# A four-layer graph network on one core: units of two slots of seven destination tiles in place of groups of four slots of one tile

## What is computed

```
layer 0: two graph attentions (4 heads, self loops added):
    e = leaky_relu(alpha_s[src] + alpha_d[dst]); softmax of e over the edges of each dst
    out[dst] = sum of alpha * h[src] + bias          (elu between the two)
layer 1: relu(x W_self + b) and relu((sum of weight * x[src] by dst) W_neigh + b), normalized, added
layer 2: attention with q, k, v (8 heads) over the same edges and loops, batch norms, feed-forward
layer 3: e = (h[dst] - h[src]) theta + h[src] phi; relu(bn(e)); e fc1; relu(bn(e)); mean over the edges of dst; relu(x + h)
```

## Time and profile before

| what | us |
| --- | --- |
| median of three runs (lowest, highest) | 13634.71 (13632.43, 13640.51) |
| profiled execution, its span | 15925.7 |
| order_nodes, build_slots (0 to 1190) | 696 and 494 |
| first gather pass, layer 0 (1369 to 4600) | 3231 |
| second gather pass, layer 0 (4725 to 7944) | 3219 |
| layer 1 and the setup of layer 2 (7944 to 9142) | 1198 |
| third gather pass, layer 2 (9142 to 11728) | 2586 |
| fourth gather pass, edge_stats (12207 to 14745) | 2538 |
| edge_spread (14745 to 15197) | 452 |
| edge_mean (15197 to the end) | 729 |

### The profile page before, as it was taken

One profiled execution on the slowest core, in us unless ns is written; L12 is line 12 of the kernel. 1 busy time (PEld: TensorE's weight loads), 2 busy tenths in 40 slices (PEclk: granted clock), 3 DMA queues, 4 the chain that ended last, 5 costly groups with the idle time before them and its releaser, 6 DMA issues. The chain is left out here.

```text
span 15925.7 us, 135557 instructions
## 1 busy us (share of the span) xinstructions
PE 3804.3 (24%) x15373; PEld 2322.4 (15%) x15374; DVE 8054.8 (51%) x18639; ACT 2750.8 (17%) x7793; POOL 7318.6 (46%) x7722
## 2 busy tenths in 40 slices
PE   2011112122221112222268200000032111111876
PEld 1001111111221111111234100000011111111321
DVE  8663555555644555555620466666653333333754
ACT  0410222222321222222300000000000000000754
POOL 0105554555545555555400266666623666666024
PEclk9996555555555555555689555555565555555999
DMA  0002222223322222223345133333311332333754
GB/s 2 14 23 48 65 65 69 71 69 76 76 64 63 63 71 64 69 75 76 79 178 219 37 93 93 93 93 95 96 37 52 91 90 89 92 89 89 245 183 147
DMA packets 977545, 1355.17 MB, mean 85 GB/s; under 512 B 223796, under 2 KB 654618, under 8 KB 964536
## 3 DMA queue, kind: packets, MB, share of 16 engines
q0 software_dynamic: 262304, 622.51, 15.4%
q1 hardware_dynamic: 226200, 403.02, 7.7%
q10 hardware_dynamic: 488960, 328.91, 7.1%
HBM read 1006.43 MB, written 347.39 MB: 85 GB/s over the span
## 5 line engine op out<-in xcount | busy, mean ns | idle before, releaser
L819 POOL DMA_INDIRECT ring<-gat_table,index x3424 | 3332.4, 973 | 2981.8 <-POOLq L102 1999.4
L819 POOL DMA_INDIRECT ring<-kv_table,index x1712 | 1693.3, 989 | 868.9 <-issue 431.8
L819 POOL DMA_INDIRECT ring<-b_table,index x1712 | 1629.3, 952 | 956.4 <-issue 522.3
L1045 DVE TENSOR_REDUCE acc<-prod 128x132 f32<-128x660 f32 (+1 forms) x1284 | 1708.0, 1330 | 5.0
L949 PE MATMUL pairs<-hot_lo,hot_hi 128*128 128x128 f32 x6272 | 961.8, 327 | 2317.5 <-ACT hot_lo L976 2070.7
L1033 DVE TENSOR_TENSOR prod<-ring,p 128x528 f32<-128x528 f32 (+1 forms) x1284 | 916.5, 714 | 963.7 <-issue 711.0
L976 ACT ACTIVATE hot_lo<-hot_lo,wt 128x128 f32<-128x128 f32 x3136 | 951.2, 392 | 2021.9 <-DVE hot_lo L929 1699.4
L949 PEld LDWEIGHTS pairs<-hot_lo,hot_hi 128*128 128x128 f32 x6272 | 931.7, 240 | 2375.5 <-issue 2373.5
L1105 ACT ACTIVATE p<-x 128x20 f32<-128x20 f32 (+1 forms) x1284 | 290.7, 226 | 5217.6 <-DVE x L1051 4105.7
L943 PE MATMUL pairs<-nil 128*128 128x512 bf16 x784 | 390.3, 598 | 2790.8 <-issue 1763.5
L1637 PE MATMUL bt<-ident,ring 128*128 128x128 f32 x1712 | 464.9, 427 | 2060.9 <-PEq L102 738.3
(11 more groups left out here) (358 smaller groups left out, 8692.7 us busy)
## 6 DMA issues: line engine op xcount, KB each, us to landing
dense_weights<-dstage ACTq DMA_DIRECT2D x196, 1024.0 KB
mat<-dense_weights SPq DMA_DIRECT2D x98, 1568.0 KB
kept<-tb ACTq DMA_DIRECT2D x432, 256.0 KB
layer_out<-kept SPq DMA_DIRECT2D x428, 256.0 KB
at<-kept SPq DMA_DIRECT2D x428, 256.0 KB
ring<-gat_table,index POOLq DMA_INDIRECT x3424
ring<-kv_table,index POOLq DMA_INDIRECT x1712
ring<-b_table,index POOLq DMA_INDIRECT x1712
```

The costliest lines, as they stand in the source:

```text
L819: pool.indirect_dma_start(self.ring[:, r * J + j, :], None, self.table, bass.IndirectOffsetOnAxis(self.index[:, half, at:at + 1], 0)).then ...
L1045: return dve.tensor_reduce(acc[:, :], prod[:, :, :].rearrange("p s c -> p c s"), AX.X, ALU.add)
```

## The change

Seven tiles form a **band** (NB = 7 bands). A **unit** is S = 2 slots of all seven tiles: UG = 14 gathers, slot by slot. A band has as many units as its highest degree needs, at least seven; the total is rounded up to 4n + 2. The ring holds RU = 4 units (56 gathers). Indices are loaded two units at a time, in three parts of the partitions. `attention_pass` treats a unit in one go: the loop that had the scores of one group beside the products of the one before is replaced by a straight order, and the sum of five by three additions and products over 924 columns (952 in layer 2, where the product with the query is written over the keys in the ring). The dense chunks of layer 0 stand inside the band: each tile's chunk comes ahead of that tile's share of the units (`beside`), its nine waits are two, and the drain behind it is gone. ACT takes a tile's chunk, the exponents of its units, and then its store.

In layer 3 a unit of 917,504 bytes is turned, kept and loaded again, with two buffers (`KeptUnits`) in place of eight; its statistics go over four quarters of 448 columns, and `edge_mean` sums straight into a band's `acc`, so that fold and transpose come once a band. `build_slots` runs over bands and writes `slot_src` in three parts and `turned` in two ("kept edge rows" for up to 160 units; `Regathered` stays for more).

```
-J = 4
-R = 4
-RING = 2 * R
+S = 2
+UG = S * B7
+RU = 4
...
-GMAX = E // J + 4 * T + T * GC + 2 * GC
-CAP = 512
+UMAX = E // S + 256
+CAP = 160
...
 class Gather:
...
+        self.ring = s.sb("ring", [P, RU * UG, width])
...
+            claim(pool, self.i_sem[half], 16 * len(SPARTS))
+            for r in range(half * 2, half * 2 + 2):
+                claim(pool, self.used)
+                for i in range(UG):
+                    at = (r % 2) * UG + i
+                    pool.indirect_dma_start(self.ring[:, r * UG + i, :], None, self.table,
...
 class DenseRows:
...
-        with dve.Fori(c0, c0 + n):
-            take(dve, self.col_in, 16)
-            for b in range(QUADS):
-                take(dve, self.used[b])
+        with dve.Fori(0, n):
+            claim(dve, self.col_in, 32)
+            claim(dve, self.used, QUADS)
...
-            c(dve.drain())
-            c.reset()
...
 def attention_pass
...
+            def unit(u):
+                claim(dve, ga.landed)
+                got = ga.unit(u)
+                for f in scores(dve, got, e[:, 0:S, :], work):
+                    c(f())
+                c(dve.tensor_reduce(newmax[:, :], e[:, :, :].rearrange("p s h -> p h s"), AX.X, ALU.max))
...
                 claim(dve, p_ready)
...
-                dve.tensor_tensor(by_head(prod[:, 0:J, :]), by_head(ga.group(g)[:, :, 0:VB]),
-                                  p5[:, 0:J, :].unsqueeze(3).broadcast_to([P, J, heads, dim + 1]),
+                dve.tensor_tensor(by_head(prod[:, :, :]), by_head(got[:, :, 0:VB]),
+                                  weight[:, 0:UG, :].unsqueeze(3).broadcast_to([P, UG, heads, dim + 1]),
                                   ALU.mult).then_inc(ga.used, 1)
...
+                c(dve.tensor_tensor(by_head(acc[:, :, :]), by_head(acc[:, :, :]),
+                                    weight[:, UG:UG + B7, :].unsqueeze(3).broadcast_to([P, B7, heads, dim + 1]),
+                                    ALU.mult))
+                c(dve.tensor_tensor(prod[:, 0:B7, :], prod[:, 0:B7, :], prod[:, B7:UG, :], ALU.add))
+                dve.tensor_tensor(acc[:, :, :], acc[:, :, :], prod[:, 0:B7, :], ALU.add)
...
-            def add_up():
-                return dve.tensor_reduce(acc[:, :], prod[:, :, :].rearrange("p s c -> p c s"), AX.X, ALU.add)
...
+                    with dve.Fori(b * B7, b * B7 + B7) as t:
+                        rows_of.dve_tile(dve, parts.value())
...
+                        with dve.Fori(u, u + many) as v:
+                            unit(v)
...
-                if rows_of is not None:
-                    rows_of.dve_tile(dve, t)
...
 def edge_stats
...
-        tb = s.sb("tb", [P, R, J * P])
...
+        tb = s.sb("tb", [P, 2, S, W7])
...
-        kept = dram("kept", (CAP + R, P, J * P))
+        kept = dram("kept", (CAP + 2, P, S * W7))
```

More of the change, by code:

```diff
@@ L212, in order_nodes @@
         ti = s.sb("ti", [P, T], I32)
+        band, cnt, run = (s.sb(n, [P, NB]) for n in ("band", "cnt", "run"))
+        bi = s.sb("bi", [P, NB], I32)
+        share, edge = s.sb("share", [P, NB, B7]), s.sb("edge", [P, NB, B7 + 1], I32)
         hist, pre, tots = s.ps("hist", [P, T]), s.ps("pre", [P, T]), s.ps("tots", [P, T])
@@ L337, in _ @@
             dve.wait_ge(md_ready, 1)
[L339 to L368, removed]
@@ new lines, in _ @@
+            c(dve.tensor_tensor(cnt[:, NB - 1:NB], rank[:, 0:1], run[:, NB - 1:NB], ALU.subtract))
+            c(dve.tensor_copy(k.units[:, :], cnt[:, :]))
+            each = cnt[:, :].unsqueeze(2).broadcast_to([P, NB, B7])
+            c(dve.tensor_scalar(k.empty[:, :].rearrange("p (b w) -> p b w", w=B7), each, float(S), None, ALU.mult))
+            c(dve.tensor_tensor(k.empty[:, :], k.empty[:, :], k.deg[:, :], ALU.subtract))
+            c(dve.tensor_tensor(share[:, :, 0:B7], each, k.ramp[:, 0:B7].unsqueeze(1).broadcast_to([P, NB, B7]),
+                                ALU.mult))
@@ L939, in pe @@
         with pe.Fori(0, T) as t:
[L940 removed]
+            n = self.chunks(pe, t)
             for b in range(QUADS):
@@ L1925, in act, with pe_own, pe_unit @@
-    def act(self, act):
-        n = act.value_load(self.k.total[0:1, 0:1], min_val=1, max_val=GMAX)
+    def pe_own(self, pe):
+        take(pe, self.r_ready)
+        for h in range(2):
+            mm = pe.matmul(self.e1[:, h, 0:QW], self.fc[:, :], self.r[:, h * QW:(h + 1) * QW], start=True, stop=True)
+        mm.then_inc(self.e1_ready, 1)
+    def pe_unit(self, pe):
+        for j in range(S):
+            take(pe, self.staged)
+            for w in range(B7):
+                mm = pe.transpose(self.bt[:, w * P:(w + 1) * P], self.stage[:, w, :], self.k.ident[:, :])
+            mm.then_inc(self.turned, 1)
+            self.pe_own(pe)
@@ new lines, in pe_turn, with dve_rows @@
+            def pe_turn(self, pe, a):
+                claim(pe, self.band_done)
+                claim(pe, self.o_free)
+                for w in range(B7):
+                    mm = pe.transpose(o[:, w, :], acc[:, a, w * P:(w + 1) * P], k.ident[:, :])
+                mm.then_inc(self.turned, 1)
+            def dve_rows(self, dve, c, b):
+                rows7, own = y[:, ds(b * B7, B7), :], x[:, ds(b * B7, B7), :]
+                share = rcnt[:, ds(b * B7, B7)].unsqueeze(2).broadcast_to([P, B7, D])
@@ L2147, in _, with unit @@
                 c = Chain(dve, ch)
-                def groups(first, last, q):
-                    with dve.Fori(first, last) as g:
+                def unit(a):
+                    for q in range(2 * S):
                         claim(dve, product)
-                        dve.sem_inc(source.tb_free, 1)
+                        if q == 2 * S - 1:
+                            dve.sem_inc(source.tb_free, 1)
                         dve.sem_inc(source.r4_free, 1)
```

1055 lines of the change are left out of this document (525 added, 530 removed).

## The result

The changed kernel takes 14,930.9 us (median of 4 runs, 14,914.2 to 14,957.5) against 13,637.6 before: a ratio of 1.095, 95% interval 1.0935 to 1.0966. The forecast was slower, 14,287 us, with a range to 14,850; the time lies 81 us above the range. Its profiled execution has a span of 14,912.4 us, within 0.2% of the runs: the 2,291 us by which the profile of before exceeds its runs have no counterpart here.

A forecast was written before the change was run, and what follows sets the result against it. POOL's gathers were taken to bound the four passes, with stalls only about 574 us in a run. Added gathers +540, stalls -434, lock +596 and other stages -50 made +652 on 13,635: 14,287 us, range 13,500 to 14,850.

The forecast's parts named there:

- the lock: Gather passes: a gather starting while VectorE runs a product with two SBUF operands waits for that product's end; new loss 780 us.
- the second loss: First two passes: behind `prod`, a gather start may meet the third 1.12 us product, costing 0 or 0.93, weighed a quarter.
- the work and load of a buffer: edge_spread and edge_mean: load 3.0 to 4.5 us, work some 3.8 us, taken as 4.2 us a unit.
- The frame: Four gather passes: the profile's extra 2,291 us is stalls; runs take 9,283 us there, with only 574 us stalled.
- Rival A: Gather passes: the profile's extra time lies in the 0.30 us gaps, so the kernel gets faster, some 12,100 us; chance 14%.
- +540 for added gathers: Four gather passes: 1,820 gathers a pass against 1,712, at 1.25 us each, if POOL is the bound: +540 us.
- -434 for stalls: Gather passes: 574 us of stalls removed, 140 us added for first and last units of the passes: -434 us.
- +596 for the lock: First three passes: longer two-operand products delay gathers by 780 us, the old 184 gone: +596, bounds +200 and +1,220.
- The row product: First two passes: `prod` of 2.08 us delays the gather it catches by 0.71 to 1.96 us, 1.33 in the middle.
- -50 for the other stages: Outside the passes: build_slots -50, edge_spread +123 to 575 us, edge_mean -127 to 602: -50, bounds -250 and +200.
- Rival C: Gather passes: every unit meets the third product and all gathers under a dense chunk, +1,220, giving 14,911 us; chance 12%.
- Rival B: Gather passes: long gathers belong to two very long products alone; no change, 13,691 or 13,507 us; chance 8%.

The follow-up runs named there:

- e3: Changed kernel with edge_spread and edge_mean loading kept units in halves through five buffers instead of whole units through two: 14,369.1 us, 562 less.

## Why the prediction was wrong

The direction was right, and so was the mechanism of the largest loss, the lock; the size was not: +652 us forecast, +1,296 measured. Two terms were mis-sized: the second loss in a unit of the first two passes, and the work and load of a buffer in the edge stages. By its steps:

- **The frame.** That the profile's 2,291 us extra stand on the stalls at the tiles' ends, and that the runs have only some 574 us of them, fits: POOL no longer stops, and by this sum the runs gained little by it. The stages that the change left alone are as long in both profiles (layer 1 and the setup of layer 2: 1,198 and 1,197 us), so the excess is not spread over the execution. Rival A (the 0.30 us gaps are the profile's) is out: the fourth pass takes 2,355 us at 1,820 x 1.249 = 2,273 us of gathers, in a profile as long as the runs. That the stalls of before are the profile's was not tried by an experiment; it rests on this sum. The traces do show what the stalls are made of. This is one instruction of VectorE's queue, the one that clears a semaphore behind a wait, in the first pass before and in the whole changed kernel (count, ns shortest/median/longest, first and last start):

```profile
L96 DVEq EVENT_SEMAPHORE_RANGE_CLEAR  x441: 2/690/717, 1494.3 to 4566.5; - x147
```

```profile
L101 DVEq EVENT_SEMAPHORE_RANGE_CLEAR  x390: 54/54/55, 12.6 to 10987.8; - x195
```

Before, the 21.55 us of the earlier trace rows are largely filled with such queue instructions of VectorE, ScalarE and SyncE at some 0.70 us each. In the four passes 5,232 of them take 0.6 to 0.8 us and cover 3,096 us; in the changed kernel 205 do. Why they are slow, and whether they are so in a run, no run here tells.
- **+540 for added gathers.** Right; 1,820 a pass and gaps of 0.304 us as before.
- **-434 for stalls.** Nearly right. Beside the gathers' 9,095 us and their lengthening of 938, the four passes hold 209 us of ends and start-up stops where I had put 140.
- **+596 for the lock.** Right in kind, too small: 938 us of lengthening in place of 780. The step that failed is the second loss in the first two passes. I had laid the products end to end, put the next gather's start at the end of the first of the three and the one after at the start of the third, and gave that a quarter. In fact VectorE starts a product 0.08 us before the record of the one before ends, so that it is the second of the three, the addition of the two slots, that the gather meets, 0.06 us after its start: 0.94 us in 128 units of 130. That it hangs on some tens of ns was right, as the third pass shows, where the same gather went free. Measured 2.37 us a unit against 1.7. The row product was right (1.36 and 1.40 against 1.33), the third pass nearly (2.39 against 2.6), and the dense chunk no more than I had put (12 and 6 us a pass, where 1.7 - 1.33 - 0.23 = 0.14 us a unit makes 18): gathers and the pairs of comparisons fell into step at 1.25 us, the first of a pair taking 0.72 us in place of 0.68.

```profile
2080.18 0.94 POOL L851 DMA_INDIRECT ring<-gat_table,index  x1 [0.30 <-issue]
2081.42 0.94 POOL L851 DMA_INDIRECT ring<-gat_table,index  x1 [0.30 <-issue]
...
2080.18 0.72 DVE L962 TENSOR_TENSOR hot_hi<-hi,ramp 128x512 f32<-128x512 f32 x1
2080.82 0.68 DVE L964 TENSOR_TENSOR hot_lo<-lo,ramp 128x512 f32<-128x512 f32 x1
2081.43 0.72 DVE L962 TENSOR_TENSOR hot_hi<-hi,ramp 128x512 f32<-128x512 f32 x1
```

- **-50 for the other stages.** The step that failed most: +318 measured. build_slots came out as put (435 us, -59). edge_spread was put at 575 us and took 790, edge_mean at 602 and took 779. The form of the sum, a buffer's load and work for two units, is what the round of edge_spread shows; both terms were too small. The load was put at 3.0 to 4.5 us and measured 4.74, the work at 3.8 and measured 6.77: 5.75 us a unit in place of the 4.2 that I took. The 3.8 was too low by its own rows, which give 4.0, and the earlier trace rows has two records to a group's product (x856 for 428 groups), which makes 4.5, near the 4.74 of the rounds at the higher clock. The other 2.0 us are the lower clock: the rows are durations at a granted clock of 0.93, and I kept them for a stage in which, by the same sum, TensorE stands idle for a load in every round. The rounds of edge_mean were not followed; e3 gave back 240 us there.
- **Rival C** gave 14,911 us, near the measured time, but not by what happened: it met one of its two conditions in the first two passes, by the second of the three products in place of the third; the dense chunks cost almost nothing, and most of what was missing lay in the edge stages. That it came so near is luck. Rival B is out by the gathers' mean of 1.11 us.

Of the 644 us between forecast and result 368 are the stages outside the passes, edge_spread and edge_mean above all, 158 the lock, 69 the ends of the passes; the rest, 49, is rounding of the frame and the difference of profile and runs.

## What to carry to other kernels

- When POOL issues gathers without a stop, count the VectorE operations with two operands in SBUF. One longer than the gathers' pace (2.08 against 1.25 us) caught a gather in nearly every unit; one of 1.12 us caught one in nearly every unit or in none, by a few hundredths of a us. Keep one operand in PSUM: the gathers then kept to 945 ns.
- Longer units and fewer buffers change which engine waits. Where TensorE then waits, cost its work at the lower clock, or keep more loads on their way: five half units in place of two whole ones, in a tile that was there already, gave back 562 us here.
- A large stall in a profile is a prize only if the runs have it too: compare the profile's span with the runs before counting on it.

## What the runs showed of the hardware

- A gather holds or loses the lock at its start. Of two gathers around the same addition, the one that started 0.01 us after it ran its 0.94 us, and the one that started 1.25 us after it waited to its end. Of those that met the addition of the two slots, 256 that started 0.05 to 0.07 us after it took some 1.88 us, and 129 that started 0.02 to 0.04 us after it some 0.95.
- The loser is not always POOL: under the dense chunks the first comparison of a pair (128x512) went from a mean of 686 ns in the kernel before to 710, and nearly all gathers there kept their length. That it waits for the gather is inferred from the two starting together.
- A weight load of 128x128 took 0.34 us after a pause of 3.74 us and 0.19 us later in the same round, at granted clocks of 0.50 and 1.00.
